# Layer norm statistics moved behind the additions of the stage ahead, and eight norms without constant products ahead of their first turn

## The reference

```
def _layernorm(x, axis=-1, eps=1e-05):
    m = jnp.mean(x, axis=axis, keepdims=True)
    v = jnp.var(x, axis=axis, keepdims=True)
    return (x - m) / jnp.sqrt(v + eps)
...
    x = x + _L0_xattn_ref(_layernorm(x, axis=-1), ctx_1024, ctx_1024, L0_xattn_w_q, L0_xattn_w_k, L0_xattn_w_v, L0_xattn_w_o)
...
    x = x + _L3_ffn_ref(_layernorm(x, axis=-1), L3_ffn_weight_q, L3_ffn_weight_scale, L3_ffn_bias)
```

## Time and profile before

| | us |
|---|---|
| median of 3 executions | 3613.26 |
| lowest, highest | 3611.83, 3616.99 |
| the profiled execution, device time | 3608.83 |
| its span in the trace | 3607.0 |
| PE busy in it (share of the span) | 3381.5 (94%) |
| DVE busy in it (share) | 2091.1 (58%) |
| ACT busy in it (share) | 1719.2 (48%) |
| granted TensorE clock, mean over the span | 0.974 |

### The profile page before, as it was taken

The page is one execution under the profiler, slowest core; times in us unless marked ns, Lnnn a source line. Parts: engine busy times, 40 slices in busy tenths (PEclk is TensorE's granted clock), DMA queues, the critical chain, the costliest instruction groups (busy, mean ns, idle before and its releaser), DMA issues. The chain is left out here.

```text
span 3607.0 us, 91217 instructions
## 1 busy us (share of the span) xinstructions
PE 3381.5 (94%) x39608; PEld 2382.1 (66%) x39608; DVE 2091.1 (58%) x4136; ACT 1719.2 (48%) x3158; POOL 817.4 (23%) x464
## 2 busy tenths in 40 slices
PE   7999999979998979999989998999999789999996
PEld 4777777656676658888854455777777565665554
DVE  5666666754444257777654484556656456555337
ACT  4777777623332168887645452444444342112124
POOL 2776777410110000000031121011010003331002
PEclk9999999999999999999998999999999889999998
DMA  2111111030101415354010002112110002320530
GB/s 78 45 39 39 39 50 46 6 99 29 38 1 50 161 48 177 111 174 166 2 42 24 0 0 70 41 41 60 41 59 23 25 15 93 109 99 12 178 126 17
DMA packets 154953, 223.35 MB, mean 62 GB/s; under 512 B 39327, under 2 KB 134235, under 8 KB 154428
## 3 DMA queue, kind: packets, MB, share of 16 engines
q1 hardware_dynamic: 154556, 217.51, 18.2%
HBM read 216.44 MB, written 1.05 MB: 60 GB/s over the span
## 5 line engine op out<-in xcount | busy, mean ns | idle before, releaser
L3361 POOL TENSOR_TENSOR x_sc<-x_sc,h_T 128x2048 f32<-128x2048 f32 (+1 forms) x105 | 443.6, 4269 | 199.1 <-ACT h_T L3588 199.1
L3171 ACT ACTIVATE x_sc<-x_sc,x_nb 128x2048 f32<-128x2048 f32 (+1 forms) x112 | 210.6, 1880 | 297.5 <-DVE x_sc L3220 297.3
L3220 DVE SCALAR_TENSOR_TENSOR x_sc<-ps,x_nb,x_cap 128x2048 f32<-128x2048 f32 (+1 forms) x112 | 246.2, 2198 | 49.1 <-PE ps L3112 49.1
L3663 DVE TENSOR_TENSOR x_most<-x_most,ps 128x512 f32<-128x512 f32 (+1 forms) x352 | 234.9, 685 | 46.5 <-PE ps L3478 34.1
L1795 ACT ACTIVATE s1i_both<-ps,s_less,s_rs_s 128x64 f32<-128x64 f32 x624 | 215.0, 427 | 48.6 <-DVE s_less L1912 48.6
L3567 ACT COPY x_sc<-ps 128x1024 f32<-128x1024 f32 x192 | 179.4, 945 | 111.4 <-PE ps L3478 71.3
L3581 ACT ACTIVATE x_sc<-x_sc 128x2048 f32<-128x2048 f32 (+1 forms) x112 | 200.8, 1797 | 3.7 <-DVE x_sc L3361 3.7
L3434 PE MATMUL ps<-x_wv,x_ctx_T 128*128 128x256 f32 (+1 forms) x832 | 201.4, 383 | 0.0
L3083 PE MATMUL ps<-x_ctx_T,x_wk 128*128 128x401 f32 (+1 forms) x512 | 200.0, 517 | 1.5 <-PEq L44 1.5
L3426 PE MATMUL ps<-x_ctx_T,x_wk 128*128 128x401 f32 (+1 forms) x512 | 196.6, 522 | 4.5 <-POOL x_v L3390 3.8
L3091 PE MATMUL ps<-x_wv,x_ctx_T 128*128 128x256 f32 (+1 forms) x832 | 197.7, 379 | 0.0
(11 more groups left out here) (563 smaller groups left out, 7051.8 us busy)
## 6 DMA issues: line engine op xcount, KB each, us to landing
x_ctx_T<-in_ctx_T SPq DMA_DIRECT2D x32, 1601.0 KB
s1i_ctx_T<-in_ctx_T SPq DMA_DIRECT2D x16, 1601.0 KB, 7.1
x3i_ctx_T<-in_ctx_T SPq DMA_DIRECT2D x16, 1601.0 KB, 7.4
s1i_ctx_n<-in_ctx SPq DMA_DIRECT2D x16, 1536.0 KB
x3i_ctx_n<-in_ctx SPq DMA_DIRECT2D x16, 768.0 KB
h<-in_ctx SPq DMA_DIRECT2D x12, 896.0 KB
e_w<-in_L_attn_W SPq DMA_DIRECT2D x8, 1024.0 KB, 7.5
rows<-in_ctx SPq DMA_DIRECT2D x12, 640.0 KB
```

The costliest lines, as they stand in the source:

```text
L3171: nc.scalar.activation(x, x, ACT.Square, scale=DH ** -0.5, bias=nb[0:keys, 0:1]).then_inc(squared, 1)
L3220: nc.vector.scalar_tensor_tensor(out=slot[0:keys].rearrange("p r m h j q -> p (r m h) (j q)")[:, :, 0:width], in0=score_banks[0:keys].rear ...
L3361: return eng.tensor_tensor(x, x, most_of, ALU.subtract)
L3663: ins = nc.vector.tensor_tensor(best[0:keys, rs], best[0:keys, rs], score_banks[0:keys, rs, :, j, :], ALU.max)
```

## The change

`measure_x` is a wait for additions to `x` to be written and then `bn_stats` of the tiles given. It is put behind the last additions to each tile in the stages ahead of e0_in, f0, s1, g1, x2, a2, f2, x3, a3 and q, mostly for tile t - 1 behind the addition to tile t, and for the last tile behind everything. These ten norms begin with `bn_aggr` of all eight tiles. ACT takes both square roots ahead of its four tiles. Eight of them (f0, s1, g1, x2, a2, f2, x3, a3) do no constant product ahead of the first turn; e0_in keeps its four, x0 and a1 stay as they were. `prime_root` does a square root of one column at the end of ACT's list in the stage ahead, so that the table load stands there. It is at the end of seven of the stages that do such a load later, and in `project_blocks`.

```
+def measure_x(nc, env, dve, added, count, tiles):
+
+    dve.wait_ge(added, count)
+    for t in tiles:
+        nc.vector.bn_stats(env.bn[:, t, :], env.x[:, t, :])
+
+
+def prime_root(nc, env):
+
+    env.primes += 1
+    nc.scalar.activation(env.primed[:, env.primes:env.primes + 1], env.eps5[:, 0:1], ACT.Sqrt)
...
-    BUSY_AHEAD = 3 if dst_T is not None else 4
+    BUSY_AHEAD = (0 if measured else 3) if dst_T is not None else 4
...
                 def aggregate(half):
-                    steps.wait()
+                    if not measured:
+                        steps.wait()
...
-                measure(range(HALF))
+                if not measured:
+                    measure(range(HALF))
                 aggregate(0)
...
-                measure(range(HALF, HALF + 1))
+                if measured:
+                    aggregate(1)
+                else:
+                    measure(range(HALF, HALF + 1))
                 invert(0)
...
-                measure(range(HALF + 1, T))
-                aggregate(1)
+                if not measured:
+                    measure(range(HALF + 1, T))
+                    aggregate(1)
...
                 deviations(0)
+                if measured:
+                    deviations(1)
                 act.wait_ge(shift_ready, 1)
                 for t in range(HALF):
-                    if t == HALF - 1:
+                    if t == HALF - 1 and not measured:
                         deviations(1)
```

In the stages ahead, four of the ten places (L0 FFN, L1 FFN, L0 cross-attention, L2 attention):

```
                                 op1=ALU.add).then_inc(added, 1)
+                            if e == order[-1] and kind == "down" and j > 0:
+                                measure_x(nc, env, dve, added, plan.down_count(item, j - 1),
+                                          [t - 1])
+                        if e == order[-1] and kind == "down":
+                            measure_x(nc, env, dve, added, plan.down_count(item, 3), [t])
...
                                         ALU.add).then_inc(dve_taken, 1)
+                                measure_x(nc, env, dve, dve_taken, plan.taken(slot)[1],
+                                          [2 * b, 2 * b + 1])
...
                                             ALU.add).then_inc(added, 1)
+                    if t > 0:
+                        measure_x(nc, env, dve, added, t, [t - 1])
                 for f in last_fillers:
                     divide(f)
+                measure_x(nc, env, dve, added, T - 1, [T - 2])
                 dve.wait_ge(projected, T)
                 nc.vector.tensor_tensor(env.x[:, T - 1, :], env.x[:, T - 1, :],
                                         product_of(T - 1), ALU.add).then_inc(added, 1)
+                measure_x(nc, env, dve, added, T, [T - 1])
...
                                                 ALU.add).then_inc(added, 1)
+                        if t > 0:
+                            measure_x(nc, env, dve, added, t, [t - 1])
+                        if t == T - 1:
+                            measure_x(nc, env, dve, added, T, [t])
```

More of the change, by code:

```diff
@@ L79, in wview, with layernorm @@
     return ap.rearrange("(k p) n -> p k n", p=P)
-def layernorm(nc, env, stage, src, nat, dst_T, loads=(), begun=(), first=None):
+def measure_x(nc, env, dve, added, count, tiles):
[5 more added lines that the diff above has]
+    nc.scalar.activation(env.primed[:, env.primes:env.primes + 1], env.eps5[:, 0:1], ACT.Sqrt)
+def layernorm(nc, env, stage, src, nat, dst_T, loads=(), begun=(), first=None, measured=False):
     HALF = T // 2
     SPARE_BANK = 7
-    BUSY_AHEAD = 3 if dst_T is not None else 4
+    BUSY_AHEAD = (0 if measured else 3) if dst_T is not None else 4
     with signals(nc, stage, "loaded own stats std shift_ready rows_act rows_dve turned act_out "
@@ L546, in _ @@
                     act_part(act, item, own, product, hidden)
+                prime_root(nc, env)
             @block.vector
@@ L789, in l0_attn @@
             att_in, ffn_in = (att0, att1), (ffn0, ffn1)
-            layernorm(nc, env, "e0_in", env.x, env.h, None,
+            layernorm(nc, env, "e0_in", env.x, env.h, None, measured=True,
                       begun=[(dst, src, att0) for dst, src in loads_att(0)], loads=[
@@ L1162, in finish @@
                                                         env.h[:, t, :], ALU.add).then_inc(final, 1)
+                                if t > c * HALF:
+                                    measure_x(nc, env, dve, final, t, [t - 1])
+                            measure_x(nc, env, dve, final, t + 1, [t])
                         begin(0)
@@ L1355, in l0_ffn @@
         with signals(nc, "f0_in", "in_even in_odd out_even out_odd") as landed:
-            layernorm(nc, env, "f0_ln", env.x, env.h, env.h_T, loads=[
+            layernorm(nc, env, "f0_ln", env.x, env.h, env.h_T, measured=True, loads=[
                 (gate[:, :, :], wview(d["L0_ffn_gate_w"])), (b1[:, :, :], d["L0_ffn_b1"]),
@@ L1500, in slots_out @@
                 return slot[pair % LANES][:, :, :]
-            layernorm(nc, env, "s1_ln", env.x, env.h, env.h_T)
+            layernorm(nc, env, "s1_ln", env.x, env.h, env.h_T, measured=True)
             with signals(nc, "s1_pre", "own product combined ssq_cleared") as (
@@ L2308, in add @@
                                             ).then_inc(added, 1)
+                    if t >= 3:
+                        measure_x(nc, env, dve, added, t, [0, 1, 2] if t == 3 else [t - 1])
+                    if t == T - 1:
+                        measure_x(nc, env, dve, added, T, [t])
                 for n in range(T + OUT):
@@ L2513, in l1_ffn @@
         with signals(nc, "g1_in", "first_in later_in pads") as (first_in, later_in, pads):
-            layernorm(nc, env, "g1_ln", env.x, env.h, env.h_T,
+            layernorm(nc, env, "g1_ln", env.x, env.h, env.h_T, measured=True,
                       begun=[(dst, src, first_in) for dst, src in first])
@@ L3760, in _ @@
                     last.then_inc(product, 1)
+            @block.scalar
+            def _(act):
+                prime_root(nc, env)
             @block.vector
@@ L3788, in _ @@
                         nc.vector.memset(wo[:, :, :], 0.0).then_inc(cleared, 1)
-            layernorm(nc, env, "x2_ln", env.x, env.h, env.h_T, loads=[
+            layernorm(nc, env, "x2_ln", env.x, env.h, env.h_T, measured=True, loads=[
                 (ctx_T[0][:, :, :], wview(d["ctx_T"][0])),
@@ L3827, in l2_attn @@
         ps = env.ps
-        layernorm(nc, env, "a2_ln", env.x, env.h, env.h_T, loads=[
+        layernorm(nc, env, "a2_ln", env.x, env.h, env.h_T, measured=True, loads=[
             (w_qk[:, :, 0, :], wview(d["L2_attn_Wq"])), (w_qk[:, :, 1, :], wview(d["L2_attn_Wk"])),
@@ L4169, in l2_ffn @@
         with signals(nc, "f2_in", "in_even in_odd out_even out_odd") as landed:
-            layernorm(nc, env, "f2_ln", env.x, env.h, env.h_T, loads=[
+            layernorm(nc, env, "f2_ln", env.x, env.h, env.h_T, measured=True, loads=[
                 (gate[:, :, :], wview(d["L2_ffn_gate_w"])),
@@ L4353, in take @@
                                     ).then_inc(added, 1)
+                                if n == X - 1 and t > 0:
+                                    measure_x(nc, env, dve, added, T * n + t, [t - 1])
+                            if n == X - 1 and j == T - 2:
+                                measure_x(nc, env, dve, added, T * X, [T - 1])
                         def combine(n, x):
@@ L4513, in l3_xattn @@
             WIDTH = 2 * P
-            layernorm(nc, env, "x3_ln", env.x, env.h, env.h_T)
+            layernorm(nc, env, "x3_ln", env.x, env.h, env.h_T, measured=True)
             linear_T(nc, env, "x3_q", [(env.h_T, given.wq, q_T, given.bq, None)])
@@ L4705, in add @@
                         def add(n):
+                            if n > 0:
+                                measure_x(nc, env, dve, added, n, [n - 1])
                             dve.wait_ge(o_done, n + 1)
@@ L4736, in l3_attn @@
         causal = sb("causal", [P, P])
-        layernorm(nc, env, "a3_ln", env.x, env.h, env.h_T, loads=[
+        layernorm(nc, env, "a3_ln", env.x, env.h, env.h_T, measured=True, loads=[
             (rel_bd[:, :, :], d["rel_bd"]), (onehot[:, :, :], d["buckets"]),
@@ L4843, in _ @@
                     steps = Steps(dve, own)
-                    def measure(ts):
-                        for t in ts:
-                            steps.done(nc.vector.bn_stats(env.bn[:, t, :], env.x[:, t, :]))
                     def aggregate(h):
-                        steps.wait()
                         for t in tiles[h]:
@@ L4883, in quantise @@
                                                     ).then_inc(clipped, 1)
-                    measure(tiles[0])
                     aggregate(0)
-                    measure(tiles[1][0:1])
+                    aggregate(1)
                     invert(0)
-                    measure(tiles[1][1:])
-                    aggregate(1)
                     invert(1)
@@ L4964, in build @@
```

(1 more changed line is left out.)

## The result

| | before | after |
|---|---|---|
| median (lowest, highest), 6 executions each | 3611.88 (3608.66, 3616.99) | 3625.17 (3614.31, 3629.05) |
| the profiled execution | 3608.83 | 3614.31 |
| its granted clock | 0.974 | 0.969 |

The ratio is 1.003, with a 95% interval of 1.0018 to 1.0042: slower by 0.3%, and the interval leaves out no change. The profiled execution was the shortest of its six. It lies 5.5 above the profiled one of before (forecast +7.4), while the medians lie 13.3 apart. Most of what follows is about that difference.

A forecast was written before the change was run, and what follows sets the result against it. PE, busy nearly the whole span, bounds the kernel; time is won only where it idles or runs at half clock. 3608.8 + 10.3 - 1.4 - 1.5 = 3616.2 profiled, 4.4 below the median forecast 3620.6; range 3613 to 3628.

The forecast's parts named there:

- Statistics on the path, +10.3: Stages ahead of the ten norms: 33 moved statistics lie on the path and add 10.3; the other 47 hide in waits.
- The four boundaries, -1.5: Norms s1, f0, f2, x3: each boundary takes 9.0 with the clock falling; +0.4, -1.5, -0.1, -0.3, together -1.5.
- rival 1: The clock holds in s1 and x3, which take 7.0 in place of 9.0: 3616.6; chance 0.15.
- rival 2: Clock returns only behind the turns: 9.9 per norm in the four boundaries, 3.6 more, 3624.2; chance 0.17.
- No constant products: Four norms: PE idles 4.9 in s1, clock falls, half clock lasts 4.3 and costs 2.1; counted within the net -1.5.
- q, -1.4: Last stage, q: shorter by 1.4 as its statistics leave the chain.
- Table load, 0: ACT's table load moved to the end of the stage ahead, where ACT has long been idle: counted 0.
- Norms with loads, 0 gained: Five norms whose end SP's transfers set (x2, a3, a2, g1, e0_in): removing statistics gains nothing there.
- Rival 3: Ten stages' ends: statistics are free because another engine or fixed delay holds the barrier; sum -2.9, 3610.3; chance 0.10.

The follow-up runs named there:

- products_back: The changed kernel with the three constant products ahead of the first turn again in eight norms, statistics still moved: 3626.26, ratio 1.0041 against before.
- p_tail: p_none plus four constant products in the last three rounds of the L2 attention: 3606.61, ratio 0.9981 against before.
- p_none: Before without the constant products in eight norms, no statistic moved; products_only's instructions measured again: 3609.72, ratio 0.9990 against before.
- p_prime: p_none with only the table load moved to the end of ScalarE's list in the stages ahead, no statistic moved: 3609.68.
- products_only: Before without the constant products ahead of the first turn in eight norms, nothing else changed: 3602.63, ratio 0.9973 against before.
- half_ahead: Changed kernel, but only tiles 0 to 3 measured ahead of f0, s1, f2, x3, q; two constant products; other norms as before: 3611.72, ratio 0.9992.
- p_half: p_none with statistics of tiles 0 to 3 alone moved ahead of f0, s1, x3 and q: 3604.02, ratio 0.9980 against before.

## Why the prediction was right or wrong

*The number.* 3620.6 was 4.6 under the median, inside the range, with the right sign. As a difference the forecast was +7.4, and measured were +13.3 between the first medians and +10.7 (±1.1) between the means of all executions. The profiled execution was 1.9 under its forecast of 3616.2. That closeness is in part luck: two errors that follow were of opposite sign, statistics dearer by 5.6 and products whose absence won 2.4 more than was forecast, together the 3.3 from 7.4 to 10.7. The terms that the trace of before gave were good, and what was missing is something that they could not give.

*Statistics on the path, +10.3.* Right in its places and sizes. In the profile PE's or DVE's wait ahead of the norm grew by 1.28 in f0 (predicted 1.3), 0.96 in s1 and 0.97 in x3 (1.0), 0.64 in g1, a2 and q (0.7), 0.45 in a3 (0.45), 0.77 and 0.73 in x2 (1.6 together). In the L2 attention three rounds lengthened by 0.33 and the end by 0.65: 1.6 for 1.7. Only e0_in is off: 0.7 + 0.45 for 1.2, as predicted, and 1.1 more because PE did its last eight products partly at half clock.

*What the step left out: the clock ahead of and behind the norm.* The prediction let the statistics lengthen PE's idle time and counted the clock's fall in the norms alone, and there as an effect of the missing products. products_back showed that the statistics lower the clock with the products in place (0.9674 against 0.9708), and that the products run partly at half behind 3.07 of idle time. In the L2 attention the stretch from a2 to f2 has a mean of 112.1 in the four profiles with the change's statistics in its loop and 107.3 in the eight without any and without p_tail's products: 4.8 (±1.2), with 8.4 more at half clock. Of that 1.6 is the statistics' own. But single profiles without statistics lie between 103.0 and 109.4, so the part above 1.6 rests on few. This is the term that was mis-sized: 14.1 measured for the statistics, where the prediction's own terms, with the products kept, come to about 8.5 (10.3 - 1.4 in q - 0.4 in s1, from 3.24 to the 2.81 of the products). By the fit half of the 14.1 is clock (7.0) and half is not.

*The four boundaries, -1.5.* 8.36, 9.58, 8.39 and 8.91, together 35.2 for a forecast of 36.0. The clock fell in all four, so rival 1 did not come. How long half clock lasted differed: in s1 to the last turn, as rival 2 had it (9.9), in x3 for most of the turns, in f0 and f2 for about half of them. The rule of the Trainium skill (TensorE: Matmul & The Clock Gate, Part 1: The HAM clock gate) that activity releases the throttle is borne out in the order of events, in s1 late and in f0 early. As an argument against dropping the products it holds for these four boundaries while the statistics are in the norm (see the next point), and not for the kernel: dropping them won 6.1 (±1.3).

*No constant products.* The prediction's net made them worth about 1.0 of gain. They are worth 6.1 (±1.3) without the statistics and 3.4 (±2.1) with them. Six products at half clock hold the first turn until 5.25 from the norm's start, as the earlier trace rows show; that was read as f0's own case, with smaller shares in f2 and x3. With the statistics moved this is what counts: the four boundaries f0, s1, f2 and x3 take 38.6 together in products_back and 35.2 and 35.1 in the changed kernel's two profiles, 3.4 to 3.5 less. With the statistics in the norm it is the other way round. The first turn can't come before 3.24, and without products it comes at half clock. Norm s1 in p_none, for the earlier trace rows:

```profile
1281.18 1.41 DVE L141 BATCH_NORM_STATS2 bn<-x 128x6 f32<-128x256 f32 x4 [1.20 <-PEq L44]
1284.43 0.69 PE L225 MATMUL ps<-consts,h 128*128 128x128 f32 x2 [5.36 <-ACT h L200]
1290.79 1.53 PE L1557 MATMUL ps<-s1i_both 128*128 128x256 f32 x6 [1.07 <-PEq L44]
```

This boundary takes 9.61 (before 8.61), and the four take 40.4 to 42.5 in the profiles of p_none, p_prime and products_only, against 37.5 in before. So the 6.1 are not won there. The profiles show two places where they may be: the stage behind a3, whose first products take 5.0 less (for 0.4 to 1.0 more in the norm), and the stretch from g1 to x2, 323.1 to 325.1 in the seven profiles without products and without statistics ahead of x2, against 325.7 in before and 325.8 in half_ahead. That this makes up the 6.1 is not shown, since only one or two executions of each list were traced.

*q, -1.4.* From its start to the end it took 24.9 before and 23.5 after.

*Table load, 0.* Right as far as it can be told: p_prime and p_none have the same median, with the means 1.4 (±2.1) apart.

*Norms with loads, 0 gained.* Right for the norms themselves (SP still waits 5.7 and 6.6). But the prediction stopped at the end of the block. Behind a3 the changed kernel's first products take 15.5, as they do in before, while 10.5 was to be had with the products gone and the statistics left alone: what one part of the change could win there the other lost. So the sum came out right at a3 for a reason that it did not have.

*Rival 3*, free statistics at the stages' ends, falls by its own point: norm starts stayed 0.7 to 1.24 behind DVE's last end.

*What stays open.* The changed kernel's profiled executions (3614.3, 3618.0) were the shortest of theirs, and the others of the two sets 11.4 and 6.2 longer in the mean, at clocks of 0.963 to 0.968. In which stages they lose is not seen in any trace.

**A faster version.** p_none (6.1 ±1.3 under before, all executions) and p_half (8.5 ±1.5) beat both kernels. p_half keeps the part of the idea that pays: only statistics that stand in a wait for products, none behind the last addition, and no constant products. Their difference, 2.4, is not shown.

## What to carry to other kernels

Work that is taken out of a boundary and put directly ahead of its barrier is not gone from the chain; move only as much as fits in waits that exist (here tiles 0 to 3, which wait for products anyway). Price idle time of TensorE around a boundary by the clock too: by the fit it was half of what the statistics cost here (7.0 of 14.1). Whether filler products pay depends on what comes next. Where the first real product could start ahead of their end, they held it up (38.6 against 35.2 at four boundaries); where it could not, they cost nothing and the turns ran quicker behind them (37.5 against 40.4 or more). And where a transfer sets the end of a stage, look at the clock of the stage behind it: behind norm a3 it made 5.0.

## What was not expected of the hardware

The same instruction list took 22.7 us in four profiles and 27.3 to 27.8 in four others at the end of the L2 attention, with granted clocks of 0.77 and 0.57, and the first 48 products behind norm a3 took 10.5 or 15.5; and executions of one kernel spread over 19 us (3604.1 to 3622.8 for before) along one line: 2.08 us for each 0.001 of mean clock. One profile of a kernel, and even nine executions, can mislead by 3 to 5 us: two sets of executions of the same list stood 9.5 and 3.8 under before, each with a 95% interval of about ±4.
